# Statistics and read of g by halves of a group, and xb of the next group made behind its first r_hi, in a hypergraph block on one Trainium2 core

## What is computed

```python
def hypergraph_conv(x, adj, W, b):
    H = (adj != 0)
    w = adj[:, 0, :]
    xw = x @ W.T
    Dn = 1 / (H @ w)                      # 0 where the sum is 0
    Be = 1 / H.sum(axis=1)
    m = Be[:, :, None] * (H.T @ xw)
    return Dn[:, :, None] * (H @ m) + b

h = relu(hypergraph_conv(x, adj, W1, b1))
h = layer_norm(h, gamma, beta)            # over 512 features
y = hypergraph_conv(h, adj, W2, b2)
out = normalise(x + (y + x))              # over 256 features, no weights
```

## Time and profile before

| | us |
|---|---|
| median of 3 runs | 303.43 |
| lowest, highest | 302.49, 303.74 |
| the profiled execution | 302.48 |
| its span in the trace | 300.6 |

### The profile page before, as it was taken

The page is one execution under the profiler, slowest core; times in us unless marked ns, Lnnn a source line. Parts: engine busy times, 40 slices in busy tenths (PEclk is TensorE's granted clock), DMA queues, the critical chain, the costliest instruction groups (busy, mean ns, idle before and its releaser), DMA issues.

```text
span 300.6 us, 5790 instructions
## 1 busy us (share of the span) xinstructions
PE 285.8 (95%) x1866; PEld 253.5 (84%) x1866; DVE 208.4 (69%) x587; ACT 212.6 (71%) x621; POOL 126.6 (42%) x163
## 2 busy tenths in 40 slices
PE   7799999999999999999999999999999999999991
PEld 6689879798988979898897989889797988979790
DVE  2788496785758577585858758594866859385784
ACT  3497869688585968858596886859688685755514
POOL 2236162707245270714527171543617063362462
PEclk9999999999999999999999999999999999999998
DMA  7920500505133050603315060311405210020104
GB/s 223 293 67 20 159 0 17 177 1 164 31 88 107 20 173 2 182 13 91 101 28 167 2 193 0 113 47 20 142 1 157 73 50 22 0 72 1 70 2 140
DMA packets 33510, 24.27 MB, mean 81 GB/s; under 512 B 7932, under 2 KB 33224, under 8 KB 33480
## 3 DMA queue, kind: packets, MB, share of 16 engines
q1 hardware_dynamic: 33376, 23.86, 26.7%
q10 hardware_dynamic: 104, 0.04, 0.1%
HBM read 13.80 MB, written 8.39 MB: 74 GB/s over the span
## 4 chain that ended last, share of the span: by engine, by line
PE 40%; DVE 16%; POOL 16%; ACT 15%; issue 11%; DVEq 0%; POOLq 0%
PE bank_v L259 10%; PE bank_v L308 10%; POOL rstd L844 7%; ACT ht_sb L429 5%; DVE bn_sb L684 5%; PE bank_s L238 5%; POOL rstd L866 5%; DVE g_sb L641 5%; PE bank_v L274 4%; ACT scratch L488 4%; ACT r_sb L466 3%; POOL r_hi L859 3%; PE bank_g L301 2%; PE bank_g L284 2%; PE bank_g L291 2%
## 5 line engine op out<-in xcount | busy, mean ns | idle before, releaser
L284 PE MATMUL bank_g<-w_hi,r_hi 128*128 128x258 f32 x256 | 65.5, 288 | 0.0
L286 PE MATMUL bank_g<-w_lo,r_hi 128*128 128x256 f32 x256 | 63.8, 282 | 0.0
L866 POOL TENSOR_TENSOR rstd<-var,half_power 128x4 f32<-128x4 f32 (+1 forms) x17 | 17.7, 1043 | 105.8 <-DVE var L698 105.8
L650 DVE TENSOR_TENSOR r_lo<-r_sb,r_hi 128x512 fp32r<-128x512 f32 x64 | 42.7, 688 | 27.5 <-POOL r_hi L859 27.5
L859 POOL TENSOR_SCALAR r_hi<-r_sb 128x512 fp32r<-128x512 f32 x64 | 40.8, 638 | 35.0 <-ACT r_sb L466 35.0
L466 ACT ACTIVATE r_sb<-bank_v,vec 128x512 f32<-128x512 f32 x64 | 44.1, 689 | 11.8 <-PE bank_v L274 11.2
L274 PE MATMUL bank_v<-u_hi,w_hi 128*128 128x512 f32 x128 | 50.7, 396 | 0.4 <-DVE u_lo L610 0.4
L274 PE MATMUL bank_v<-u_hi,w_lo 128*128 128x512 f32 x128 | 50.8, 397 | 0.0
L274 PE MATMUL bank_v<-u_lo,w_hi 128*128 128x512 f32 x128 | 50.6, 396 | 0.0
L284 PEld LDWEIGHTS bank_g<-w_hi,r_hi 128*128 128x128 f32 x256 | 48.3, 189 | 1.4
L286 PEld LDWEIGHTS bank_g<-w_lo,r_hi 128*128 128x128 f32 x256 | 48.2, 188 | 1.2
(11 more groups left out here) (98 smaller groups left out, 464.8 us busy)
## 6 DMA issues: line engine op xcount, KB each, us to landing
x_sb<-in_x_dram SPq DMA_DIRECT2D x16, 512.0 KB, 3.9
out_dram<-z_sb SPq DMA_DIRECT2D x15, 512.0 KB, 3.2
adj_sb<-in_adj_dram SPq DMA_DIRECT2D x16, 256.0 KB, 3.8
w_raw<-in_L_gnn_W_dram SPq DMA_DIRECT2D x2, 512.0 KB, 5.5
out_dram<-z_sb SPq DMA_DIRECT2D x2, 256.0 KB, 2.5
turned_h<-h_sb SPq DMA_TRANSPOSE x13, 2.4
b_half<-in_L_gnn_b_dram SPq DMA_DIRECT2D x1, 128.0 KB, 9.0
edge_rows<-in_adj_dram ACTq DMA_DIRECT2D x1, 32.0 KB, 3.3
```

What stands on the lines that cost most here:

```text
L284: pe.matmul(bank_g[:, n, 0:W2COLS], r_hi[:, i % 2, k, graph(n)], w2_hi[:, k], start=(k == 0), stop=False)
L286: pe.matmul(bank_g[:, n, 0:DOUT], r_hi[:, i % 2, k, graph(n)], w2_lo[:, k], start=False, stop=False, skip_group_check=True)
L650: nc.vector.tensor_tensor(r_lo[:, i % 2, k], r_sb[:, k], r_hi[:, i % 2, k].bitcast(F32), ALU.subtract).then_inc(r_lo_ready, 1)
```

## The change

sum_q steps q_summed behind each half. make_g steps g_made behind graphs 1 and 3. make_var1, inverse_std1 and read_g are called by halves in every group. On VectorE the first half's var1 and read_g stand ahead of make_var2(i-1), and the second half's read_g stands right behind its var1, ahead of split_r(i+1, 1) and the pair. On GpSimd the first half's inverse_std1 is ahead of inverse_std2(i-1), and add_b2(i+1) moves from behind split_r(i+1, 2) to right behind split_r(i+1, 0), with a wait for VectorE's r_lo of the same chunk; the second half's inverse_std1 stays behind split_r(i+1, 1). add_b2(15) had its own place behind a wait on q_ready and is now inside the loop. The counts of all waits follow.

```diff
@@ -139,7 +139,7 @@
         stats_ready, mean2_ready = sem("stats_ready"), sem("mean2_ready")
         var2_ready, rstd2_ready, shift2_ready = sem("var2_ready"), sem("rstd2_ready"), sem("shift2_ready")
         out_ready, last_out_ready = sem("out_ready"), [sem("last_out_low"), sem("last_out_high")]
-        last_q_half, last_shift2_ready = sem("last_q_half"), sem("last_shift2_ready")
+        last_shift2_ready = sem("last_shift2_ready")
 
         def graph(n):
             return slice(n * P, (n + 1) * P)
@@ -277,7 +277,7 @@
 
             def make_g(i, n):
                 if n == PER - 1:
-                    pe.wait_ge(q_summed, i + 1)
+                    pe.wait_ge(q_summed, 2 * i + 2)
                 for k in range(KH):
                     if n == 0:
                         pe.wait_ge(r_hi_ready, i * KH + (k + 1))
@@ -290,12 +290,12 @@
                         pe.wait_ge(r_lo_ready, i * KH + (k + 1))
                     mm = pe.matmul(bank_g[:, n, 0:W2COLS], r_lo[:, i % 2, k, graph(n)], w2_hi[:, k], start=False,
                                    stop=(k == KH - 1))
-                if n == PER - 1 or (i == LAST and n == PER // 2 - 1):
+                if n % 2:
                     mm.then_inc(g_made, 1)
 
             def turn_q(i):
                 pe.wait_ge(q_ready, i + 1)
-                pe.wait_ge(q_summed, i)
+                pe.wait_ge(q_summed, i * 2)
                 pe.wait_ge(g_ready, i * 2)
                 for n in range(PER):
                     mm = pe.transpose(turned_q[:, graph(n)], q_sb[:, graph(n)], ident[:, :])
@@ -406,7 +406,7 @@
                 elif n == 2:
                     pe.wait_ge(at_ready, G)
                 else:
-                    pe.wait_ge(q_summed, G)
+                    pe.wait_ge(q_summed, G * 2)
                 pe.matmul(last_z[n], ident_2[:, :], xb_sb[:, 1, n], start=True, stop=False)
             for half in range(2):
                 pe.wait_ge(g_ready, LAST * 2 + half + 1)
@@ -483,13 +483,12 @@
             def sum_q(i):
                 act.wait_ge(q_turned, i + 1)
                 if i:
-                    act.wait_ge(var1_ready, i)
+                    act.wait_ge(var1_ready, i * 2)
                 for n in range(PER):
                     ins = nc.scalar.activation(scratch[:, n], turned_q[:, graph(n)], ACT.Copy,
                                                accum_out=sum_sq[:, n:n + 1])
-                    if i == LAST and n == PER // 2 - 1:
-                        ins.then_inc(last_q_half, 1)
-                ins.then_inc(q_summed, 1)
+                    if n % 2:
+                        ins.then_inc(q_summed, 1)
 
             def normalise_last():
 
@@ -610,18 +609,15 @@
                     nc.vector.tensor_tensor(u_lo[:, c], bank_v[:, c], u_hi[:, c].bitcast(F32),
                                             ALU.subtract).then_inc(u_lo_ready, 1)
 
-            def make_var1(i, half=None):
-                part, done = graphs(half), i + (half or 0)
+            def make_var1(i, half):
+                part, done = graphs(half), i * 2 + half
                 dve.wait_ge(g_made, done + 1)
                 nc.vector.tensor_scalar(stat1[:, 0, part], bank_g[:, part, SUM], 1.0 / HID, None,
                                         ALU.mult).then_inc(stat1_step, 1)
                 dve.wait_ge(stat1_step, done * 3 + 1)
                 nc.vector.tensor_tensor(stat1[:, 1, part], stat1[:, 0, part], stat1[:, 0, part],
                                         ALU.mult).then_inc(stat1_step, 1)
-                if half == 0:
-                    dve.wait_ge(last_q_half, 1)
-                else:
-                    dve.wait_ge(q_summed, i + 1)
+                dve.wait_ge(q_summed, done + 1)
                 dve.wait_ge(stat1_step, done * 3 + 2)
                 nc.vector.scalar_tensor_tensor(out=stat1[:, 2, part], in0=sum_sq[:, part], scalar=1.0 / HID,
                                                in1=stat1[:, 1, part], op0=ALU.mult,
@@ -630,23 +626,22 @@
                 nc.vector.tensor_scalar(stat1[:, 3, part], stat1[:, 2, part], 0.0, EPS, ALU.max,
                                         ALU.add).then_inc(var1_ready, 1)
 
-            def read_g(i, half=None):
+            def read_g(i, half):
                 if i == 0:
                     dve.wait_ge(c2_ready, 1)
                 else:
                     dve.wait_ge(y_made, i * 2)
-                dve.wait_ge(rstd1_ready, i + (half or 0) + 1)
-                for h in range(2) if half is None else (half,):
-                    for n in each(h):
-                        ins = nc.vector.scalar_tensor_tensor(out=g_sb[:, n], in0=bank_g[:, n, 0:DOUT],
-                                                             scalar=rstd1[:, n:n + 1], in1=c2[:, :],
-                                                             op0=ALU.mult, op1=ALU.add)
-                    ins.then_inc(g_ready, 1)
+                dve.wait_ge(rstd1_ready, i * 2 + half + 1)
+                for n in each(half):
+                    ins = nc.vector.scalar_tensor_tensor(out=g_sb[:, n], in0=bank_g[:, n, 0:DOUT],
+                                                         scalar=rstd1[:, n:n + 1], in1=c2[:, :],
+                                                         op0=ALU.mult, op1=ALU.add)
+                ins.then_inc(g_ready, 1)
 
             def split_r(i, k):
                 dve.wait_ge(r_hi_ready, i * KH + (k + 1))
                 if i >= 2:
-                    dve.wait_ge(g_made, i - 1)
+                    dve.wait_ge(g_made, (i - 1) * 2)
                 nc.vector.tensor_tensor(r_lo[:, i % 2, k], r_sb[:, k], r_hi[:, i % 2, k].bitcast(F32),
                                         ALU.subtract).then_inc(r_lo_ready, 1)
 
@@ -778,16 +773,19 @@
                         make_b(i + 3)
                     take_stats2(i - 1, 0)
                     take_stats2(i - 1, 1)
+                make_var1(i, 0)
+                read_g(i, 0)
+                if i:
                     make_var2(i - 1)
                     if i + 4 < G:
                         make_h(i + 4)
                 split_r(i + 1, 0)
-                make_var1(i)
+                make_var1(i, 1)
                 if i == 0:
                     make_b(3)
+                read_g(i, 1)
                 split_r(i + 1, 1)
                 add_pair(i + 1, 0)
-                read_g(i)
                 if i + 1 < LAST:
                     make_z(i, 0)
                     make_z(i, 1)
@@ -838,9 +836,9 @@
                 nc.gpsimd.tensor_copy(htb_sb[:, j % 2, :, P],
                                       edge_cols[:, j * PER:(j + 1) * PER]).then_inc(wcol_ready, 1)
 
-            def inverse_std1(i, half=None):
+            def inverse_std1(i, half):
                 part = graphs(half)
-                pool.wait_ge(var1_ready, i + (half or 0) + 1)
+                pool.wait_ge(var1_ready, i * 2 + half + 1)
                 nc.gpsimd.tensor_tensor(rstd1[:, part], stat1[:, 3, part], half_power[:, part],
                                         ALU.pow).then_inc(rstd1_ready, 1)
 
@@ -855,7 +853,7 @@
             def split_r(i, k):
                 pool.wait_ge(relu_ready, i * KH + (k + 1))
                 if i >= 2:
-                    pool.wait_ge(g_made, i - 1)
+                    pool.wait_ge(g_made, (i - 1) * 2)
                 nc.gpsimd.tensor_scalar(r_hi[:, i % 2, k], r_sb[:, k], 1.0, 1.0, ALU.mult,
                                         ALU.mult).then_inc(r_hi_ready, 1)
 
@@ -904,17 +902,16 @@
             for i in range(LAST):
                 if i + 3 < G:
                     copy_w(i + 3)
+                inverse_std1(i, 0)
                 if i:
                     inverse_std2(i - 1)
                 split_r(i + 1, 0)
+                pool.wait_ge(r_lo_ready, (i + 1) * KH + 1)
+                add_b2(i + 1)
                 split_r(i + 1, 1)
-                inverse_std1(i)
+                inverse_std1(i, 1)
                 split_r(i + 1, 2)
-                if i + 1 < LAST:
-                    add_b2(i + 1)
                 split_r(i + 1, 3)
-            pool.wait_ge(q_ready, G)
-            add_b2(LAST)
             for half in range(2):
                 inverse_std1(LAST, half)
             inverse_std2(LAST - 1)
```

## The result

| | median, us | profiled execution, us | span, us | ratio to before, 95% interval |
|---|---|---|---|---|
| before | 303.02 (4 runs) | 302.48 | 300.6 | |
| changed | 349.39 (347.89 to 350.96, 4 runs) | 350.21 | 348.3 | 1.1529 [1.1465, 1.1593] |

Slower by 15%, inside the predicted range (343 to 358), 1.6 us from the forecast.

What follows compares the result with a forecast made beforehand. The prediction took the kernel as a loop TensorE nearly fills, so later releases are paid each group. Its terms, 3.0 + 12 x 3.4 + 2.2 + 2.3 = 48.3 us on 302.48, gave 350.8, forecast as a 351.0 median, range 343 to 358.

Steps and rivals of the forecast that it cites:

- the four places named: TensorE idle before make_v(i+1,3), both halves of make_y and make_u, about 3.4 us together in each group.
- Order and bound: TensorE nearly fills the loop; y of half 1 comes late and make_u starts 3.4 us later each group.
- var2: On VectorE behind read_g of half 0: make_var2 takes 0.76 us and ends 2.64 later than before.
- Shared reads: VectorE steps with two SBUF inputs and GpSimd SBUF reads exclude each other; period 20.8 with this rule, 20.3 without.
- xb ahead of the pow as the main cost: On GpSimd, xb (add_b2 of the next group, 2.36 us) now stands ahead of half 1's pow: the main cost.
- Clock: TensorE's granted clock stays 1.00; a rival had it fall behind the stops, adding 26 us to 377, chance 0.03.
- Faster rival: y of half 0 no longer waits, 0.44 us a group, if the second half is in time; 297 to 300, chance 0.03.
- group 0: No stats or var2, but xb and r_hi come ahead of its second pow: + 3.0 us, ends 2.0 and 3.4.
- groups 1 to 12: The steady loop: 12 x 3.4 us, make_u later by 3.4 in each; bounds 2.9 and 3.8 a group.
- group 13: No ht and no binv, so its stats have 1.2 us to spare: + 2.2, ends 1.8 and 2.6.
- group 14 and the last: Same spare, no make_u, make_z and last var1 late, xb(15) leaves the tail: + 2.3 us, ends 1.5 and 3.0.

Runs made afterwards that it cites:

- e1: The changed kernel with xb (add_b2) of the next group put back behind GpSimd's r_hi of chunk 2; median 352.96 us.
- e5: The kernel before with only xb (add_b2) moved behind the first r_hi, with the wait for r_lo; 321.30 us, ratio 1.0616.
- e6: The changed kernel without GpSimd's wait for r_lo ahead of xb; 347.09 us.
- e7: The changed kernel with var1's second step reading one of its inputs from PSUM instead of the mean twice from SBUF; 349.84 us.
- e10: The changed kernel with xb and make_var2 put back, so only read_g of half 1 stays ahead of r_lo of chunk 1 and the pair; 341.31 us.
- e3: The changed kernel with make_var2 and make_h put back ahead of read_g of half 0; 323.52 us, ratio 1.0675.
- e12: e10 with 30 small transposes filling TensorE's stop ahead of make_u(i+2); 326.51 us, ratio 1.077.
- e4: The changed kernel with halves kept, but xb, read_g of half 1 and make_var2 put back where they stood; 297.30 us, ratio 0.982.
- e8: The changed kernel with 18 small transposes on TensorE between the halves of make_y and 12 ahead of make_u; 347.99 us, ratio 1.1495.

## Why the prediction was right, step by step

Chain by chain, in us behind turn_q (the prediction held turn_q at 131.50; in the trace after it is at 152.60):

| step | predicted | measured |
|---|---|---|
| read_g of half 0 done | 7.27 | 7.16 |
| pow of var2 starts | 8.12 | 7.80 |
| xb ends | 13.26 | 12.97 |
| second pow starts | 14.18 | 13.84 |
| y of half 1 starts | 15.95 | 15.59 |
| make_u starts | 18.05 | 17.62 |
| period | 20.8 | 20.37 |

- **Order and bound**: right in the loop. Every link came in the order walked, TensorE waits at the four places named, and y of half 1 is the late one.
- **var2**: mis-sized. I gave it 0.76, which held 0.11 of waiting for the stats; behind read_g the record of its last step ends 0.55 behind that of read_g (159.76 to 160.31). With the 0.11 by which read_g is already early, the pow starts 0.32 earlier against turn_q, most of the difference of 0.43 at make_u. The rest comes in sums of durations, since a VectorE record overlaps the next by some 0.08 (read_g ends at 159.76, the next step starts at 159.67).
- **Shared reads**: right in kind and size. e1, e5, e6, e7 and e10 each put a step with two SBUF inputs beside xb in another way, and each time it lasted till xb's end: the small steps (128x2, 128x4) ended within 0.03 of it, those of 128x512 some 0.55 behind it. The Trainium skill's rule (SBUF — State Buffer, Who interferes with whom) holds here for steps of 128x2 too (2.38 us instead of 0.16). e7 supports its other half: an input from PSUM frees the step.
- **xb ahead of the pow as the main cost**: only half right. Alone it costs 1.5 a group (e5), but undoing it alone gives nothing (e1), since xb then meets the pair. Of the three places undone alone, var2 gives most (e3, 26 us).
- **Clock**: wrong, and by the prediction's own sign ("if the granted clock falls in the loop"). I gave 1.00, and 0.03 to a fall; the row at 10 to 12 us was no guide. The stops are 0.42, 0.21, 1.23 and 0.90, 2.8 in sum where I had 3.4, and in some groups the clock fell in or behind them. The Trainium skill (TensorE: Matmul & The Clock Gate, A second HAM failure mode), with its kernel whose clock swung over short idles, was the better guide: e10 and e12 show it here (0.92 and 1.00 with the stop filled).
- **Faster rival**: its gain is real (e4: 0.4 a group), and its condition, that the second half be in time, was the one the change broke.

Term by term, between the starts of turn_q of groups 0, 1, 13 and 14 in the two traces (30.22, 44.62, 253.18, 269.81 before; 30.25, 48.88, 297.45, 315.81 after):

| part | predicted, us | measured, us |
|---|---|---|
| group 0 | 3.0 | 4.2, 1.3 of it behind a fall of the clock |
| groups 1 to 12 | 40.8 | 40.0: 35.7 at full clock, 4.3 by three falls |
| group 13 | 2.2 | 1.7 |
| group 14 and the last | 2.3 | 1.7 |
| sum | 48.3 | 47.7 |

So that the time came out within 1.6 us is in part luck. At full clock every term came out a little smaller than I had it, and the falls, which the sum had at nothing, filled 5.6 of the 47.7. Without them the same sum gives some 344.6 us for the profiled execution (an estimate from these rows), still in its range from 342.6 on, but at the low end. Group 0 came out by another path than walked: its y is 2.9 late (42.72 against 39.79) because binv stands on VectorE behind the held steps of var1, ScalarE waits 3.13 for it and relu is late; there y waits for relu last, not for g_sb. And the forecast of 351.0 does not follow from its own working, which gives 350.8 + 0.95 = 351.7.

What stays open: why the same stop of 0.90 is followed by a fall in some groups of the changed kernel and not in others, why e5's stop of 1.63 a group is never followed by one, and why e8's first turn_q is late.

## What to carry to other kernels

When a step is split in halves so that the first half is early, ask what the second half now stands behind; that half decides. Before moving a GpSimd instruction, list the VectorE steps with two SBUF inputs that will run beside it, since each, however small, can last as long as it does. A stop of 1 to 2 us in TensorE's loop can cost nearly its own length again in granted clock (e10), or nothing (e5), so read the clock row by stretches before adding up waits.

## What the runs showed of the hardware that was not expected

Behind stops of 0.9 to 2.1 us TensorE came to its 1.2 GHz level, in three of twelve groups of the changed kernel and in groups 1 to 11 of e10, where TensorE was busy 18.51 of 20.58 us (0.92 over a group, 341.31 us; with the stop filled, 1.00 and 326.51). e5 stops once a group for 1.63 us and never fell in its loop: its period stays at 18.8 to 18.9, with 1.00 from 40 to 280 us.
